# Attention and routed experts on one core: other times for eight sends and for five shift additions

## What is computed

```python
h = layernorm(x) * (1 + ca) + sa
w = exp(tanh((h @ W + b) @ h.T * lw)) * off_diag          # lw = 1/|i-j|
x = x + ga * (w / (w.sum(-1) + EPS)) @ h
h = layernorm(x) * (1 + cb) + sb
logits = h @ Wg;  top_vals, top_idx = top_k(logits, 2);  top_w = softmax(top_vals)
sparse = sum over the two experts of top_w * (relu(h @ W1[e] + b1[e]) @ W2[e] + b2[e])
shared = relu(h @ Ws1 + bs1) @ Ws2 + bs2
out = x + gb * (sparse + shared)
```

## Time and profile before

| | us |
|---|---|
| three runs, median | 642.19 (642.18 to 644.39) |
| the profiled execution | 641.25 |
| its span, first to last instruction | 639.5 |
| PE busy in it | 613.3 (96%) |
| DVE busy | 459.0 (72%) |
| ACT busy | 406.3 (64%) |
| POOL busy | 350.3 (55%) |

### The profile page before, as it was taken

How to read it: one execution, slowest core, us unless ns; L and a number is a source line. 1 busy time by engine, 2 the same in 40 slices (tenths; PEclk the granted TensorE clock), 3 DMA queues, 4 the chain that set the end, 5 groups by cost and what they waited for, 6 DMA issues and landing times.

```text
span 639.5 us, 13351 instructions
## 1 busy us (share of the span) xinstructions
PE 613.3 (96%) x4339; PEld 557.5 (87%) x4339; DVE 459.0 (72%) x1425; ACT 406.3 (64%) x647; POOL 350.3 (55%) x347
## 2 busy tenths in 40 slices
PE   7899999999999998969999999999999999999997
PEld 5788898788888887858999999999999999998897
DVE  7869798999989896966842676665556544452598
ACT  3698778778787876725565656665555656463551
POOL 5450526867666666665763565566656556466100
PEclk8999999999999999988999999999999999999999
DMA  7500000110111111110752555567666566521793
GB/s 295 196 14 1 2 2 18 34 35 30 34 34 35 34 35 38 39 46 25 243 168 83 180 180 182 184 187 213 182 205 192 183 189 191 177 68 31 268 403 128
DMA packets 30031, 76.46 MB, mean 120 GB/s; under 512 B 7142, under 2 KB 11646, under 8 KB 29856
## 3 DMA queue, kind: packets, MB, share of 16 engines
q1 hardware_dynamic: 20624, 58.49, 28.1%
q0 software_dynamic: 8640, 16.93, 7.9%
q10 hardware_dynamic: 720, 0.47, 0.2%
HBM read 53.53 MB, written 23.24 MB: 120 GB/s over the span
## 4 chain that ended last, share of the span: by engine, by line
PE 60%; DVE 22%; ACT 5%; issue 5%; POOL 3%; another core or an unknown queue 3%; DMA 1%; POOLq 0%; SPq 0%; DVEq 0%; ACTq 0%
PE value L2060 24%; PE score L1840 8%; PE score L1842 8%; PE score L1841 8%; PE value L1868 6%; DVE work L1238 4%; DVE rows_all L1225 2%; DVE stats L1121 2%; PE value L2108 2%; PE misc L1882 2%; ACT work L873 2%; DVE rows_all L1260 2%; ACT work L875 2%; POOL rstd L602 1%
## 5 line engine op out<-in xcount | busy, mean ns | idle before, releaser
L817 POOL DMA_INDIRECT rows_z<-tile_y,tags x138 | 142.4, 1032 | 101.1 <-issue 43.7
L1840 PE MATMUL score<-h_hi,h_lo 128*128 128x512 f32 (+1 forms) x252 | 94.4, 374 | 0.3 <-ACT work L904 0.2
L1868 PE MATMUL value<-w_ring,work 128*128 128x129 f32 x768 | 93.2, 277 | 0.8 <-ACT work L875 0.3
L1868 PEld LDWEIGHTS value<-w_ring,work 128*128 128x128 f32 x768 | 89.8, 192 | 4.7 <-ACT work L875 2.0
L873 ACT ACTIVATE work<-work 128x1024 f32<-128x1024 f32 x64 | 67.3, 1052 | 38.3 <-DVE work L1238 36.2
L1842 PE MATMUL score<-h_hi,h_lo 128*128 128x512 f32 (+1 forms) x252 | 89.4, 355 | 0.0
L904 ACT ACTIVATE work<-score,w_ring 128x512 f32<-128x512 f32 (+1 forms) x96 | 53.2, 617 | 55.7 <-PE score L1842 41.8
L622 POOL DMA_INDIRECT rows_x<-work,slot x64 | 65.7, 1027 | 35.0 <-issue 16.9
L1238 DVE TENSOR_TENSOR work<-score,lw 128x1024 f32<-128x1024 f32 x64 | 76.6, 1215 | 5.0 <-remote 2.3
L1841 PE MATMUL score<-h_hi,h_lo 128*128 128x512 f32 (+1 forms) x220 | 76.4, 347 | 0.0
L2060 PE MATMUL value<-w_ring,work 128*128 128x128 f32 x640 | 75.4, 275 | 0.0
(11 more groups left out here) (282 smaller groups left out, 1208.4 us busy)
## 6 DMA issues: line engine op xcount, KB each, us to landing
w_ring<-packs SPq DMA_DIRECT2D x24, 578.0 KB
rows_all<-packs SPq DMA_DIRECT2D x23, 578.0 KB
lw<-rows_x SPq DMA_DIRECT2D x24, 260.0 KB
res<-x SPq DMA_DIRECT2D x8, 512.0 KB, 6.5
h_t<-rows_z SPq DMA_DIRECT2D x3, 1024.0 KB, 11.7
mod<-mod_rows SPq DMA_DIRECT2D x1, 2560.0 KB, 8.8
rows_z<-tile_y,tags POOLq DMA_INDIRECT x142
rows_all<-rows_z SPq DMA_DIRECT2D x2, 1024.0 KB, 13.2
```

The lines of the kernel that those rows point to most:

```text
L817: nc.gpsimd.indirect_dma_start(rows_z[:, :], bass.IndirectOffsetOnAxis(ap=tags[pos][:, k, 0:1].bitcast(I32), axis=0), tile_y[par][:, k, :] ...
L1840: nc.tensor.matmul(out, a_lo, b_hi, start=True, stop=False)
L1868: ins = nc.tensor.matmul(value[:, s // 3, c0:c0 + D + 1], prob[:, t % 4, s * P:(s + 1) * P], normal[b % 3][:, t, :], start=(t == 0 and s % ...
```

## The change

Two things on POOL alone; the other engines' programs stay, with their lines 15 further down.

- The shift additions of b = 3, 4, 5 and 6 leave the start of their own batch and stand in the batch before, after the sends of tile 5, behind a wait (b = 3: tile 6 is weighed; the others: `ln2_h`). The one of b = 7 leaves tile 6 of batch 6 and stands in the last batch before the first send of tile 3.
- In the last batch, from tile 4 on, two sends for each tile and not three, so that batch 5 has eight sends left and not four. The 40 sends of the second part, where there were 36, get another pacing: two, two, two and one, then `rstd_2(7)`, then groups of three behind `up_ready` and `down_ready`, the last behind `down_ready` 7.

```diff
@@ -629,8 +629,7 @@
 
                 if t < FIRST:
                     return [(b - 3, 2 * G - LATE + 2 * t + i) for i in range(2)]
-                each = 2 if b < B - 1 else 3
-                return [(b - 2, each * (t - FIRST) + i) for i in range(each)]
+                return [(b - 2, 2 * (t - FIRST) + i) for i in range(2)]
 
             def send_one(b, m):
                 if exists(b):
@@ -660,36 +659,27 @@
                 pool.wait_ge(exp_done, G * b + 3)
                 send_step(b, 2, 1)
                 pool.wait_ge(score_used, G * b + 4)
+                add_shift(b)
                 send_step(b, 3, 0)
                 pool.wait_ge(exp_done, G * b + 4)
                 send_step(b, 3, 1)
-                pool.wait_ge(tanh_done, G * b + 4)
-                send_step(b, 3, 2)
                 pool.wait_ge(score_used, G * b + 5)
                 send_step(b, 4, 0)
                 pool.wait_ge(exp_done, G * b + 5)
                 send_step(b, 4, 1)
                 rstd_2(b - 1)
-                pool.wait_ge(tanh_done, G * b + 5)
-                send_step(b, 4, 2)
                 pool.wait_ge(score_used, G * b + 6)
                 send_step(b, 5, 0)
                 pool.wait_ge(exp_done, G * b + 6)
                 send_step(b, 5, 1)
-                pool.wait_ge(tanh_done, G * b + 6)
-                send_step(b, 5, 2)
                 pool.wait_ge(score_used, G * b + 7)
                 send_step(b, 6, 0)
                 pool.wait_ge(exp_done, G * b + 7)
                 send_step(b, 6, 1)
-                pool.wait_ge(tanh_done, G * b + 7)
-                send_step(b, 6, 2)
                 pool.wait_ge(score_used, G * b + 8)
                 send_step(b, 7, 0)
                 pool.wait_ge(exp_done, G * b + 8)
                 send_step(b, 7, 1)
-                pool.wait_ge(tanh_done, G * b + 8)
-                send_step(b, 7, 2)
 
             def second_batch(b):
                 rstd_2(b - 1)
@@ -711,7 +701,8 @@
                 if AHEAD <= b + 3 < B:
                     rstd_1(b + 3, b + 4)
                 pool.wait_ge(score_used, G * b + 1)
-                add_shift(b)
+                if b == 2:
+                    add_shift(b)
                 send_step(b, 0, 0)
                 pool.wait_ge(exp_done, G * b + 1)
                 send_step(b, 0, 1)
@@ -740,9 +731,12 @@
                 send_step(b, 5, 1)
                 if b < 3:
                     shift_rows(b - 1)
+                    pool.wait_ge(score_used, G * b + 7)
+                else:
+                    pool.wait_ge(ln2_h, b)
+                if b < B - 2:
+                    add_shift(b + 1)
                 pool.wait_ge(score_used, G * b + 7)
-                if b == B - 2:
-                    add_shift(b + 1)
                 send_step(b, 6, 0)
                 pool.wait_ge(exp_done, G * b + 7)
                 send_step(b, 6, 1)
@@ -762,7 +756,7 @@
             modulation()
             rstd_1(1, 2)
             batches(pool, batch)
-            order = iter([(B - 3, m) for m in range(3 * (G - FIRST), 2 * G)] + [(b, m) for b in (B - 2, B - 1) for m in range(2 * G)])
+            order = iter([(B - 3, m) for m in range(2 * (G - FIRST), 2 * G)] + [(b, m) for b in (B - 2, B - 1) for m in range(2 * G)])
 
             def send_next():
                 b, m = next(order)
@@ -772,17 +766,27 @@
                     pool.wait_ge(*((last_second, 1) if b == B - 1 else (second_rows, b + 1)))
                 scatter(b, m)
 
-            for _ in range(7):
-                send_next()
+            pool.wait_ge(value_step, G * B)
+            send_next()
+            send_next()
+            pool.wait_ge(up_ready, HALVES)
+            send_next()
+            send_next()
+            pool.wait_ge(down_ready, 1)
+            send_next()
+            send_next()
+            pool.wait_ge(up_ready, HALVES * 2)
+            send_next()
             rstd_2(B - 1)
-            pool.wait_ge(up_ready, HALVES * 3)
+            pool.wait_ge(up_ready, HALVES * 4)
+            send_next()
             send_next()
             send_next()
             pool.wait_ge(down_ready, 2)
             send_next()
             send_next()
             send_next()
-            pool.wait_ge(up_ready, HALVES * 4)
+            pool.wait_ge(up_ready, HALVES * 5)
             send_next()
             send_next()
             send_next()
@@ -790,17 +794,28 @@
             send_next()
             send_next()
             send_next()
-            pool.wait_ge(up_ready, HALVES * 5)
-            send_next()
-            send_next()
-            for n in range(4, FRONT):
-                pool.wait_ge(down_ready, n)
+            pool.wait_ge(up_ready, HALVES * 6)
+            send_next()
+            send_next()
+            send_next()
+            pool.wait_ge(down_ready, 4)
+            send_next()
+            send_next()
+            send_next()
+            for n in range(6, FRONT):
+                pool.wait_ge(up_ready, HALVES * (n + 1))
                 send_next()
                 send_next()
-                pool.wait_ge(up_ready, HALVES * (n + 2))
+                send_next()
+                pool.wait_ge(down_ready, n - 1)
                 send_next()
                 send_next()
-
+                send_next()
+            pool.wait_ge(up_ready, HALVES * (FRONT + 1))
+            send_next()
+            send_next()
+            pool.wait_ge(down_ready, FRONT - 1)
+            send_next()
 
             def send(i, pos, paced=True):
 
```

## The result

The changed kernel takes 672.49 us (median of 4 runs, 666.49 to 673.61) against 643.29 for the kernel before: ratio 1.0445, interval 1.0379 to 1.0511. The direction was forecast, the size (652.0, and 659 at the high end) was not. The profiled execution is the fastest of the four: span 664.7 us against 639.5, so the traces stand 25.24 us apart where the medians stand 29.2 apart.

A forecast was written before the change was run, and what follows sets the result against it. PE was taken as the bound (60% of the chain). Terms -1.3 + 1.85 + 7.0 + 1.7 + 0.6 = +9.85 on the profiled 641.25 us gave 651.1; with the median 0.9 above, 652.0, range 645 to 659.

The forecast's parts named there:

- Shifts of b = 3 to 6: Fourth to seventh batch: blocking of DVE goes, new places are paid; -2.4 or -0.1 us by a race, middle -1.3.
- The blocking of L1309: In b = 3 and 4, POOL's shift addition held this DVE addition; 1.89 and 1.03 us of blocking would go.
- The race of L1135: Batches 3 and 4: DVE's shift_1 against POOL's moved addition, 0.06 us apart; if POOL is first, DVE waits 2.3 us.
- Shift of b = 7: Last batch: the moved addition would hold DVE's scale_attended (L1260) 1.9 us, bounds 0 and 2.4; +1.85 in the sum.
- the rival with ACT's 9.04 us: Before the first relu at 287.03: dense sends stall PE's signals, and spreading removes it; -6.8 us, 645.2; chance 0.13.
- D: Theory from the experiments, not the prediction: while POOL issues sends in a row, PE's signals come late.
- my signs of being wrong: last_rows within 1 us of its old place relative to shared_up(3), ranks(7) without idling, or ACT's 9.04 us gone.
- The wait for the eighth send: Behind the last batch: last_rows waits for batch 5's eighth send and delays PE at ranks(7); +7.0 us (5.2 to 8.4).
- The slow clock: Behind PE's wait at ranks(7), part of the clock at 1.2 and not 2.4 GHz; +1.7 us (1.6 to 3.3).
- The last loads: After POOL's 27 sends behind shared_up(4), row tile 4's load reaches PE 0.6 us late; +0.6 us (0 to 2).
- what would show it: Listed signs: L1309, L1135 and L1260 times, batch periods, DVE idle 5 to 7 us, PE 5 to 8, clock under 1.
- The period of b = 3: Time between PE's gate logits starts: 34.02 us before, near 32.7 expected; for b = 4, 32 to 34.3.

The follow-up runs named there:

- g1: The changed kernel, unaltered, run again on another occasion beside the kernel before: 649.85 us, ratio 1.0279.
- g4: The kernel before, unaltered, run again for its trace on that other occasion: 632.63 us.
- h1: The kernel before with the shift additions of b = 3 to 6 a batch ahead, those of b = 4 to 6 behind tile 6's first send: 629.78 us, ratio 0.9963.
- g2: The kernel before with only the shift additions of b = 3 to 6 a batch ahead, run again: 632.6 us, ratio 1.001.
- e2: The kernel before with only the addition of b = 7 moved into the last batch: 649.52 us, ratio 1.0037.
- h2: The changed kernel with the eighth send of batch 5 ahead of rstd_2(7), run again on another occasion: 638.7 us, ratio 1.0094.
- e4: The changed kernel with the eighth send of batch 5 right behind the seventh, ahead of rstd_2(7): 668.51 us, ratio 1.0334.
- g3: The changed kernel with all shift additions back in their old places, so the spread sends alone: 647.29 us, ratio 1.0231.
- f3: The changed kernel with all shift additions back, the eighth send ahead of rstd_2(7), and a tail of two or three sends per group: 634.61 us, ratio 1.0043.
- e1: The kernel before with only the shift additions of b = 3 to 6 a batch ahead: 662.14 us, ratio 1.021.

## Why the prediction was wrong, step by step

The terms of the sum, measured without late signals (g1 against g4), come to 15.65 us where 9.85 was forecast; the other 9.6 of the result's 25.24 came with late signals.

- **Shifts of b = 3 to 6: -1.3, measured +0.2.** The blocking of L1309 went as forecast. The race of L1135 was lost both times (2.37 and 2.35 us in g1), by less than 0.1 us, and I had taken the middle of a coin that fell the same way in every trace with the addition in that place. The terms as I listed them give -2.3 with the race won and 0.0 to +0.25 with it lost (not -2.4 and -0.1), so the lost race was priced nearly right; the step that failed is the middle. With the addition one send later (h1) the gain is there: its span is 3.11 under g4's, of which 1.0 is an earlier start in the first batches that g2 shows too.
- **Shift of b = 7: +1.85, measured +2.7.** The held instruction is another one. In g1 the addition runs from 256.83 to 259.21 and DVE stands at L1347, ahead of scale_attended:

```profile
256.24 3.01 DVE L1347 TENSOR_SCALAR work<-token_no 128x8 int32<-128x8 f32 x1
```

  It takes 0.17 elsewhere and has one SBUF input. It started before the addition, beside the send of 255.85, and was let go when the addition ended. My sentence that DVE instructions with one SBUF tensor run on at their usual pace was wrong for this form. It is held 3.01 to 3.03 us in the result, e2 and h2 as well, and in e4 another step of its kind is (L1338, 2.59 where g1 has 0.26). The rule of the Trainium skill, page "SBUF — State Buffer", section "Who interferes with whom", names DVE instructions in a 2-port mode besides those with two inputs; that L1347 ran in such a mode no row shows.
- **The end of the last batch: not in the sum, measured -1.3.** In g4 PE's products stand at 0.63 us from 281.05 to 283.18, in g1 at 0.40; the granted clock is 0.56 from 281 to 284.5 in g4 and 1.00 from 282 to 287 in g1. In the result it is the rival with ACT's 9.04 us: that wait is gone (4.62 now), and 5.8 us came back between the eighth gate logits and the last. So this rival was right in its place and nearly in its price (6.8), and its mechanism fits D; it could not outweigh what else the change costs. That ACT's 9.04 us would go was also among my signs of being wrong.
- **The wait for the eighth send: +7.0 (5.2 to 8.4), measured +9.3.** The mechanism and place were right (in the result the term is 8.1). My own numbers give 7.2, not 7.0: 319.6 less 312.40. In g1 the send is issued at 302.48 and last_rows starts at 309.09, 6.6 later, where I took 4.4:

```profile
302.48 1.10 POOL L622 DMA_INDIRECT rows_x<-work,slot  x1 [7.27 <-PE score L1857]
```

```profile
309.09 1.23 DVE L1511 TENSOR_TENSOR rows_all<-rows_all,mod 128x1024 f32<-128x1024 f32 x1 [9.08 <-DMA rows_x<-work,slot]
```

  The weights' loads start at 300.99, 1.5 us ahead of the send, and four further sends follow it in the queue. In my nearest row, the send of 303.49, the loads started at 302.65, 0.8 ahead.
- **The slow clock: +1.7, measured +2.2.** Behind the wait the granted clock is 0.52 from 317 to 322 us in g1: nearly all at 1.2 GHz. Columns: stretch, its length, busy us of PE, its weight loads, DVE, ACT, POOL, clock, DMA share, GB/s.

```profile
317.00:322.00 5.00, 4.94 (x14) 4.13 (x15) 2.89 (x17) 1.12 (x2) 0.00 (x0) 0.52 0.00 0
```

- **The last loads: +0.6 (0 to 2), measured +2.5.** Tile 4's load starts at 360.51 in g1, 43.5 us behind ranks(7), where g4 has 33.4 (339.58 behind 306.15). PE idles 2.29 for it and goes on at full clock. The term is larger where the clock falls with it: in g3 PE idles 2.33 for the same load and goes from 11.5 to 15.6 us late, so 4.1. From 360 to 365 us, g1 and then g3:

```profile
360.00:365.00 5.00, 2.71 (x20) 2.21 (x20) 1.19 (x2) 3.54 (x6) 1.98 (x2) 1.00 0.58 158
```

```profile
360.00:365.00 5.00, 3.44 (x17) 3.45 (x18) 1.39 (x2) 2.21 (x4) 1.07 (x2) 0.66 0.81 242
```

  In h2 ranks(7) is only 3.35 late. The tiles behind it are 4.9 late, then PE idles 1.87 for that load (clock 0.66 from 355 to 360), and the rest is 8.6 late: 3.7 for the load. f3, with a lighter tail, ends 2.2 late once the 1.0 of its earlier start is added.
- **What was missed: late signals, not in the sum, 9.6 us.** I had the mechanism as a rival that could only gain, since I saw it where the kernel before suffers from it, and asked what spreading sends removes. The question left out was what the moved addition did where it stood: it kept POOL from sending for 2.4 us at the ranks. With it gone the result lost 7.8 us more than g1 by the seventh gate logits. From the third batch's gate logits to the seventh's, e1 lost 11.95 us and g2 0.15, each against the trace of before on its kind of occasion. With the heavier tail 7.11 and 8.03 us of ACT's waiting came in the first tiles. What delays the signals stays open.

Of "what would show it", L1309's length, the idling before last_rows and ranks(7) and the clock came as written. The period of b = 3 was 33.4 us (32.7 forecast), that of b = 4 34.9, above the 34.3 of a lost race.

## What to carry to other kernels

Before an instruction is moved, ask what it kept apart where it stood, not only what it blocked: here, on the occasions with late signals, e1 without the 2.4 us of work between two rows of sends lost 2%; without late signals it lost nothing. A race that 0.06 us decide isn't priced at its middle: either move the instruction out of it (one send later gained 0.4%), or count it as lost. And a queued transfer that another engine waits for must be priced with the loads that start with it. Last, take the kernel before and the changed one on one occasion: the kernel before alone differed by 2% between occasions.

## What the runs showed of the hardware

- The same kernel took 643 and 647 us on two occasions and 632.4 to 632.7 on four others; in each trace of the first kind PE's signals are late beside rows of sends, in none of the second: there 45 ranks steps with three or more sends in a row all have 0.01 us. One chip number stands under both kinds, so it is not the chip alone. The traces of the first kind also lack about half of the landings' records and a sixth of the engines' signal records that the second kind has; which comes of which, no run shows.
- Where they are late, three sends in a row are enough (1.2 to 2.1 us), and five give 2.5 to 4.1. Signals of the sends rise in between in all 15 cases, one of DVE in four and one of ACT in two; but DVE's signals were late too in one place (2.1 us, e1). What delays them, and whether another cut than the addition takes it away, stays open: the runs made for that fell on occasions without it.
- A small DVE instruction with one SBUF input only (L1347) took 3.01 to 3.03 us instead of 0.17 in four traces, from beside a send to the end of POOL's addition behind it.
